# Routed rows packed into 64 tiles with 27 extra products, and a first stage with the constants loaded behind x, four parts of blocks and normalisation by ScalarE

## The reference, cut to what matters

```python
x = L0_attn_x                                  # (8, 1024, 128) f32: 8192 tokens
xn = layernorm(x)
# "attention": out = s * colsum(W_out) + b_out for each token
off = xn @ W_off + b_off                       # only the even columns are used
w = softmax((xn @ W_attn + b_attn).reshape(..., 8, 4), axis=-1)
idx = clip(where(int(off) < 0, int(off) + 128, int(off)), 0, 127)
s = sum(take_along_axis(xn[:, 0, :], idx) * w)
# feed forward: two shared experts for all tokens, two of eight for each token
ffn = lambda x, w1, w2, w3: (silu(x @ w1.T) * (x @ w3.T)) @ w2.T   # 128 -> 256 -> 128
logits = xn @ router_w.T + expert_bias
rw, sel = top_k(logits, 2); rw = softmax(rw)
routed = sum over the two chosen experts of rw * ffn(xn, expert)
return x + attention + shared + routed
```

## Time and profile before

| | us |
|---|---|
| median of 3 runs | 506.35 (503.58 to 506.4) |
| the profiled execution | 503.18, its span 501.4 |
| PE busy | 432.6 (86%) |
| DVE busy | 331.3 (66%) |
| POOL busy | 231.1 (46%) |
| ACT busy | 229.1 (46%) |
| stage 1, first normalisation to last copy | 16.7 to 61.1 |
| stage 2, to PE's first turn of stage 3 | 61.7 to 262.4 |
| stage 3, to the last product | 262.4 to 489.4 |
| last sends | to 501.4 |

### The profile page before, as it was taken

How to read it: one execution, slowest core, us unless ns; L and a number is a source line. 1 busy time by engine, 2 the same in 40 slices (tenths; PEclk the granted TensorE clock), 3 DMA queues, 4 the chain that set the end, 5 groups by cost and what they waited for, 6 DMA issues and landing times.

```text
span 501.4 us, 14718 instructions
## 1 busy us (share of the span) xinstructions
PE 432.6 (86%) x5200; PEld 376.1 (75%) x5200; DVE 331.3 (66%) x956; ACT 229.1 (46%) x432; POOL 231.1 (46%) x179
## 2 busy tenths in 40 slices
PE   0167676677899999999999999999999999999990
PEld 0156534354577777777788999999999999999990
DVE  3799799989768799999966776344434444344440
ACT  0588841163224544444443454444444444444440
POOL 0234400146754433333000000688888888887663
PEclk9999998999999999999998999999999999999995
DMA  8999400000331111111302432354444444432000
GB/s 238 284 171 174 74 1 1 5 32 18 99 112 34 54 44 55 48 43 48 96 2 96 140 110 95 75 59 64 63 55 66 55 60 60 60 37 23 4 2 1
DMA packets 50683, 34.58 MB, mean 69 GB/s; under 512 B 9408, under 2 KB 44224, under 8 KB 50624
## 3 DMA queue, kind: packets, MB, share of 16 engines
q1 hardware_dynamic: 32048, 23.88, 20.4%
q0 software_dynamic: 15296, 8.53, 12.4%
q10 hardware_dynamic: 3280, 1.36, 1.1%
HBM read 14.87 MB, written 20.69 MB: 71 GB/s over the span
## 4 chain that ended last, share of the span: by engine, by line
PE 72%; DVE 19%; issue 2%; ACT 2%; ACTq 2%; DMA 1%; POOL 1%; DVEq 0%; POOLq 0%
PE pY L616 17%; PE pY L466 9%; PE pAB L596 9%; PE pAB L598 8%; PE pAB L597 8%; PE pAB L451 4%; PE pAB L453 4%; PE pAB L452 4%; PE pV L491 3%; PE pV L478 3%; DVE units L894 3%; PE pV L579 2%; DVE hbuf L923 2%; DVE hot L834 2%; ACTq L630 2%
## 5 line engine op out<-in xcount | busy, mean ns | idle before, releaser
L798 POOL DMA_INDIRECT out_dram<-hot,rows x92 | 142.5, 1549 | 110.9 <-DVE hot L1173 86.0
L1167 DVE SCALAR_TENSOR_TENSOR hbuf<-pAB,units 128x512 f32<-128x512 f32 x92 | 63.6, 691 | 103.9 <-PE pAB L598 103.9
L596 PE MATMUL pAB<-xT,wsp 128*128 128x128 f16 x736 | 129.6, 220 | 1.1 <-ACT xT L737 0.6
L597 PE MATMUL pAB<-xT,wsp 128*128 128x128 f16 x736 | 129.7, 220 | 0.0
L598 PE MATMUL pAB<-xT,wsp 128*128 128x128 f16 x736 | 129.6, 220 | 0.0
L788 POOL DMA_INDIRECT sorted_rows<-rows,slot x64 | 69.4, 1084 | 112.2 <-DVE hbuf L923 64.4
L616 PE MATMUL pY<-wsp,hbuf 128*128 x736 | 103.0, 282 | 1.0 <-issue 0.7
L747 ACT ACTIVATE units<-pAB 128x512 f32<-128x512 f32 x92 | 55.0, 598 | 105.5 <-PE pAB L598 105.5
L616 PEld LDWEIGHTS pY<-wsp,hbuf 128*128 128x128 f32 x736 | 89.7, 192 | 1.7 <-issue 1.3
L701 ACT ACTIVATE units<-pAB 128x512 f32<-128x512 f32 x64 | 38.1, 597 | 113.8 <-PE pAB L453 113.8
L596 PEld LDWEIGHTS pAB<-xT,wsp 128*128 x736 | 72.5, 98 | 2.6 <-issue 2.1
(11 more groups left out here) (137 smaller groups left out, 558.0 us busy)
## 6 DMA issues: line engine op xcount, KB each, us to landing
sorted_rows<-c_pad_row SPq DMA_DIRECT2D x1, 6026.0 KB, 43.7
rows<-sorted_rows SPq DMA_DIRECT2D x46, 131.0 KB, 2.2
base<-in_x SPq DMA_DIRECT2D x4, 1024.0 KB, 8.2
out_dram<-base SPq DMA_DIRECT2D x16, 256.0 KB, 2.5
wraw<-in_wall SPq DMA_DIRECT2D x8, 256.0 KB
out_dram<-hot,rows POOLq DMA_INDIRECT x92, 3.3
sorted_rows<-rows,slot POOLq DMA_INDIRECT x64
wsp<-in_wall SPq DMA_DIRECT2D x8, 128.0 KB, 2.8
```

Source lines behind the costliest of these rows:

```text
L596: pe.matmul(o, hi, x(0), start=True, stop=False)
L597: pe.matmul(o, hi, x(1), start=False, stop=False)
L798: pool.indirect_dma_start(out_rows, bass.IndirectOffsetOnAxis(ap=xr[:, t // 2 % X_RING, t % 2, DEST:DEST + 1].bitcast(U32), axis=0), yt[:, ...
L1167: v.scalar_tensor_tensor(hbuf[:, r % 4, :], pAB[:, 2 * (r % 2) + 1, :], 1 / (XS * WS), silu[:, r % 2, :], ALU.mult, ALU.mult).then_inc(d_h ...
```

## The change

The pairs of experts are put in an order in which neighbours share an expert (RUNS). Segments are no longer rounded to tiles: the 8192 rows fill 64 tiles exactly, and a tile's two products are those of the pair that owns its first row. Where a new pair begins within a tile, its one expert that the pair before lacks (COMER) is computed for that whole tile by an extra product: 27 extras, two to a job, so 14 extra jobs beside 64 main ones. Jobs run in the order main 0 to 7, extras 0 to 13, main 8 to 63. A row carries the weights of all 8 experts (ROWW 137 in place of 131), and each tile's shares are formed from them by DVE. The results of all 64 tiles stay in SBUF, cleared by POOL, and an extra adds to the tile that a register names. Sends wait for the last extra. The pad write goes. ADDS is 2, and blocks are written at WRITE_AT, which puts the last one behind turn 24 (step 34 of 78).

In stage 1, x comes in 8 DMAs on SP, the other constants and the shared weights on SP behind it; ACT issues 3 DMAs. The parts of blocks are 0-1, 2-4, 5-9, 10-15. ACT normalises all four tiles of blocks 0 to 10, DVE the fourth of blocks 11 to 15. The shared weights' split moves to blocks 14 and 15.

```diff
-NQ = 4
+NQ = 8
-TILES = -(-((TOK + NPAIR * (P - 1)) // P) // 2) * 2
-STEPS = TILES // 2
+RUNS = [(0, 1, 8), (1, 7, 8), (1, 2, 7), (2, 6, 8), (2, 3, 6), (3, 5, 8), (3, 4, 5), (4, 5, 8), (5, 7, 8), (5, 6, 7), (6, 7, 8)]
+PAIRS = [(u, v) for u, lo, hi in RUNS for v in range(lo, hi)]
+EXTRAS = NPAIR - 1
+TILES = NT
+MAIN_STEPS = TILES // 2
+XTILES = (EXTRAS + 1) // 2
-PARTS = [(0, 4), (4, 8), (8, 16)]
+PARTS = [(0, 2), (2, 5), (5, 10), (10, 16)]
-ROOT_AT = {1: 1, 2: 6}
+ROOT_AT = {1: 1, 2: 4, 3: 9}
+FOURTH_FROM = 11
-ADDS = 3
-Y_RING, OUT_SEMS = 32, 8
+ADDS = 2
+EXTRA_FROM = 8
+JOBS = ([Job(t=t) for t in range(EXTRA_FROM)] + [Job(i=i) for i in range(XTILES)]
+        + [Job(t=t) for t in range(EXTRA_FROM, TILES)])
+WRITE_AT = [min(n for n in range(AHEAD, STEPS) if FIRST_OF_TURN[n - AHEAD + 1] >= TPB * (i + 1) // ADDS + 3) for i in range(NB)]
...
 SP
-            sp.wait_ge(const_in, 16 * n_const)
-            sp.dma_start(sorted_rows..., c["pad_row"]...).then_inc(pad_out, 16)
+                if q == NQ // 2 - 1:
+                    for r in range(2):
+                        sp.dma_start(wraw[:, r, 0:W2], wall[r, :, 0:W2]).then_inc(w_in[r], 16)
+            for dst, src in [(wo[:], w_out), (bo_raw[:], ...)] + [(c[k][:], const[k]) for k in const if k != "ident"]:
+                sp.dma_start(dst, src).then_inc(const_in, 16)
...
+            def load_extra(a, landed):
+                with sp.register(f"extra{a}") as tile:
+                    sp.reg_load(tile, segi[0:1, 1, a:a + 1])
+                    ...
+                    sp.dma_start(xe[:, a - 1], sorted_tiles[bass.ds(at, 1)]...).then_inc(landed, 16)
...
+            for n, step in enumerate(TURN_ORDER):
+                if n >= AHEAD:
+                    sp.wait_ge(d_turn, n + 1 - AHEAD)
+                if step < MAIN_STEPS:
+                    sp.dma_start(xr[:, step], sorted_steps[step]).then_inc(d_in[n % AHEAD], 16)
+                else:
+                    ...load_extra for its one or two extras
+                for i in range(NB):
+                    if n == WRITE_AT[i]:
+                        write_block(i)
...
 PE
+            def spread_sides():
+                pe.wait_ge(spread_ready, 1)
+                pe.wait_ge(y_read, NB)
+                for b in range(2):
+                    mm = pe.matmul(pY[:, b, :], c["ones"][:], spread..., start=True, stop=True)
+                mm.then_inc(sides_done, 1)
...r_turn: behind turn 0
+                if job.turn == 0:
+                    spread_sides()
...r_first, r_second: as before for a main job; for an extra job
+                                e = NSH + COMER[2 * job.i + k + 1]
+                                hi, lo = (wsp[:, s, e, col + h * P:col + (h + 1) * P] for s in range(2))
...
 ACT
-            act.wait_ge(const_in, 16 * n_const)
             root(0)
+            act.wait_ge(first_in, 16 * 3)
+            nc.scalar.activation(wp[:, 0, :], wp_raw[:], ACT.Copy, scale=WS).then_inc(wp_hi, 1)
-                for j in range(TPB - 1):
+                for j in range(TPB - 1 if i >= FOURTH_FROM else TPB):
-            pipeline(act, NB, 4, 4, [(0, normalise), (0, later_roots), (0, shared_high), (2, turned_copy)])
+            pipeline(act, NB, 4, 4, [(0, normalise), (1, shared_high), (2, turned_copy), (0, later_roots)])
...
-            pipeline(act, TILES, ..., [(0, r_xt), (5, r_y_first), (2, r_silu)])
+            pipeline(act, NJOB, ..., [(0, r_xt), (2, r_silu)])
...
 POOL
+            pool.wait_ge(cw_pair, 1)
+            for m, (choice, k) in enumerate(((5, 8), (4, 9))):
+                nc.gpsimd.tensor_tensor(r8[:, choice], r8[:, choice], rt[:, k, :]..., ALU.mult).then_inc(cw_part, 1)
+            pool.wait_ge(cw_part, 2)
+            nc.gpsimd.tensor_tensor(rows32[:, :, CW:CW + E], r8[:, 5], r8[:, 4], ALU.add).then_inc(cw_ready, 1)
...behind the scatter
+            for i in range(NB):
+                pool.wait_ge(l1, 4 * i + 4)
+                nc.gpsimd.memset(yt[:, TPB * i:TPB * (i + 1)], 0.0).then_inc(y_cleared, 1)
...r_send
-                pool.wait_ge(d_y, t + 1)
+                pool.wait_ge(d_y, max(job.place, LAST_EXTRA) + 1)
...
             pool.wait_ge(out_done, 16 * NB)
-            for step in range(SEND_FROM, TILES + 7): ...
+            for job in JOBS:
+                if job.main:
+                    r_send(job)
...
 DVE, routing: L991, L993 to L997 and six of L1001 to L1007 go; seven runs of L976 become eleven
-            then(v.scalar_tensor_tensor(tab_scr[:], ... [P, 2, NPAIR] ...
+            then(v.scalar_tensor_tensor(tab_scr, ... [P, 2 + 2 * E, NPAIR] ...
...at the end of stage 2: spread_out (one tensor_tensor of 1024), extra_table (seven small ones)
...
+            def load_tiles(g, r):
+                first = REG_LOAD * (UNROLL * g + r) + 1
+                ...values_load_multi_w_load_instructions(segi[0:1, 1, first:last], engines=(DVE,), ...)
+            def side_products(g, r): (for each pair of main tiles, one tensor_tensor 128 x 32)
+            def side_sums(g, r): (one tensor_reduce of it)
+            def extra_shares(g, r): (for each extra, one tensor_tensor 128 x 1)
+            def y_first(g, r):
+                ...
+                dve.wait_ge(d_l2, q + 1)
+                if job.main:
+                    dve.wait_ge(share_ready, job.step + 1)
+                    v.scalar_tensor_tensor(yt[:, job.t], pY[:, q % 2, 0:P], share_w[:, job.t, 0:1], yt[:, job.t],
+                                           ALU.mult, ALU.add).then_inc(y_half, 1)
+                else:
+                    row = yt[:, bass.ds(extra_tile[a], 1)].rearrange("p o c -> p (o c)")
+                    v.scalar_tensor_tensor(row, pY[:, q % 2, 0:P], extra_w[:, a:a + 1], row, ALU.mult, ALU.add)...
+            def y_second(g, r): (the same for the second half, behind y_half)
-            pipeline(dve, TILES, ..., [(0, r_attention), (5, r_y), (2, r_hf)])
+            pipeline(dve, NJOB, ..., [(5, y_first), (0, r_attention), (0, load_tiles), (2, side_products), (5, y_second), (2, r_hf),
+                                      (3, side_sums), (2, extra_shares)])
```

More of the change, by code:

```diff
@@ L79, with __init__, comes_back @@
 GAP_UNIT, SEG_UNIT, TAB_UNIT, TABLE_UNIT, LOGIT_UNIT, SIZE_UNIT = 3, 6, 10, 12, 12, 14
+SPREAD_UNIT = UNITS - 4
+REG_LOAD = 4
 PACE_FROM, PACE = 9, 50
-ADDS = 3
-Y_RING, OUT_SEMS = 32, 8
-X_RING, AHEAD = NT // 2, 8
-SEND_FROM = 24
+ADDS = 2
+AHEAD, OUT_SEMS = 8, 8
+EXTRA_FROM = 8
+class Job:
+    def __init__(self, t=None, i=None):
+        self.t, self.i = t, i
+        self.main = t is not None
+        self.step = t // 2 if self.main else MAIN_STEPS + i
+        self.turns = not self.main or t % 2 == 0
+        self.experts = 2 if self.main else min(2, EXTRAS - 2 * i)
+        self.cols = self.experts * HID
+JOBS = ([Job(t=t) for t in range(EXTRA_FROM)] + [Job(i=i) for i in range(XTILES)]
+        + [Job(t=t) for t in range(EXTRA_FROM, TILES)])
+NJOB = len(JOBS)
+TURN_ORDER = [job.step for job in JOBS if job.turns]
+for n, step in enumerate(TURN_ORDER):
+    for job in JOBS:
+        if job.step == step:
+            job.turn = n
+for q, job in enumerate(JOBS):
+    job.place = q
+FIRST_OF_TURN = [min(q for q in range(NJOB) if JOBS[q].turn == n) for n in range(STEPS)]
+WRITE_AT = [min(n for n in range(AHEAD, STEPS) if FIRST_OF_TURN[n - AHEAD + 1] >= TPB * (i + 1) // ADDS + 3) for i in range(NB)]
+LAST_EXTRA = max(job.place for job in JOBS if not job.main)
+LAST_OF_TURN = [max(q for q in range(NJOB) if JOBS[q].turn == n) for n in range(STEPS)]
+def comes_back(a):
+    return max([g for g in range(a) if COMER[a] in PAIRS[g]], default=-1)
 def constants():
@@ L570, in r_turn @@
                     return
-                j = UNROLL // 2 * g + r // 2
-                pe.wait_ge(d_in[j % AHEAD], 16 * (j // AHEAD + 1))
-                if j == 0:
+                rows_landed(pe, job.step)
+                if job.turn == 0:
                     pe.wait_ge(w_split, NE)
-                if past(j, 2):
-                    pe.wait_ge(d_xt, j - 1)
-                for k in range(2):
+                if job.turn >= 2:
+                    pe.wait_ge(d_xt, job.turn - 1)
+                for k in range(2 if job.main else job.experts):
@@ L635, in _ @@
-            act.wait_ge(const_in, 16 * n_const)
-            nc.scalar.activation(wp[:, 0, :], wp_raw[:], ACT.Copy, scale=WS).then_inc(wp_hi, 1)
-            nc.scalar.copy(bo[:], bo_raw[:]).then_inc(wp_hi, 1)
+            for dst, src in [(wp_raw[:], wproj), (c["ident"][:], const["ident"]), (bp[:], bproj)]:
+                act.dma_start(dst, src).then_inc(first_in, 16)
             def split_high(g, r):
@@ L871, in _ @@
-            scales(0)
-            for i in range(*PARTS[1]):
+            for i in (3, 4):
                 block_statistics(i)
+            variances(1)
             def later_parts(g, r):
                 i = 4 * g + r
-                if i == 0:
-                    variances(1)
-                if i == 2:
+                if i == 1:
```

(34 more changed lines are left out.)

434 lines of the change are left out of this document (269 added, 165 removed).

## The result

The changed kernel takes **483.62 us** (median of 4 runs, 482.18 to 484.47) against 505.59 for the kernel before on the same chip (4 runs, 503.58 to 506.4): ratio 0.9571, 95% interval 0.9544 to 0.9598. Forecast was 473, with 467 to 478 as its own range, and 464 to 485 with the rivals. The direction was right. The time lies 10.6 us above the forecast, outside its own range and at the slow end of the wide one. Its profiled execution took 484.23 us, 1.8 more than its span of 482.4.

A forecast was written before the change was run, and what follows sets the result against it. It took DVE to bound stage 2's routing, PE the rest of stage 2 and stage 3. Stage 3's start 259.9 + last send 201.3 + tail 8.65 = 469.9 span, 471.7 time; stated 473, range 467 to 478.

The forecast's parts named there:

- ACT becomes the bound of the stage: Stage 1: ACT's work and waits give back most of a 7.1 us earlier first normalisation; last copy ends at 58.95.
- 16 of some 0.7 us are covered: End of stage 2: POOL's 16 clears of about 0.7 us each, behind the last scatter, cost nothing.
- rival 2: Stage 3 before the first send: register loads and dynamic addresses make DVE the bound, +8 to +10, 482 us; chance 0.25.
- rival 3: Stage 3: SP's register reads and DMA issues bring extra tiles late, +5 to +10, 480 us; chance 0.05.
- Stage 3, PE: PE's time from first turn to last product of stage 3 falls from 227.0 to 193.9 us.
- S: The start of stage 3, its first turn on PE, forecast at 259.9 us.
- Stage 3, the sends: POOL's 64 sends start late, run back to back at 1.85 us and set the end, adding 4.1 us.
- DVE in stage 3: DVE's new step needs 1.95 of 2.40 us, so it fits with 0.45 to spare; register loads cost nothing.
- rival 5: Stage 3: extras serialise and give back a tile's time for each saved, no change, 503 us; chance 0.03.
- rival 1: Stage 3: PE still sets the end instead of POOL's sends, 465 to 469 us; chance 0.13.
- 2.2 gained: Stage 1: the last copy ends at 58.95 instead of 61.13 us; bounds 7 gained to 2 lost.
- Rival 4: Stage 3: DVE makes PE pause in each step and PE's clock falls to 1.2 GHz, 523 us; chance 0.04.

The follow-up runs named there:

- experiment 10: Changed kernel with POOL's constants' wait behind its subtractions, clears spread between scatters, three attention additions a step, and without the 27 extra products: 440.58 us, ratio 0.8724.
- experiment 4: Changed kernel with attention added to three tiles a DVE step instead of two, last block's write behind turn 18: 479.16 us, ratio 0.9488.
- experiment 1: Changed kernel with POOL's wait for all constants, and the destination column's copy, moved behind its stage 1 subtractions: 477.62 us, ratio 0.9445.
- experiment 2: Changed kernel with POOL's 16 clears spread between the scatters of the second half instead of back to back behind the last: 477.43 us, ratio 0.9454.
- experiment 3: Changed kernel with each POOL clear waiting for the one before, all still behind the last scatter: 477.63 us, ratio 0.9439.
- experiment 6: Changed kernel with POOL's constants' wait behind its subtractions, and DVE normalising the fourth tile of all 16 blocks again: 478.72 us, ratio 0.9465.
- experiment 7: Changed kernel with the 4.5 MB pad write put back and POOL's scatter waiting for it: 484.16 us, ratio 0.9584.

## Why the prediction was right, and where it failed

**The steps that failed are "ACT becomes the bound of the stage" in stage 1 and "16 of some 0.7 us are covered" in stage 2.** They put POOL's wait for the constants and its clears at nothing, and the runs show 5.9 and 6.5 us. That the wide range still held the time was luck: its upper part stood for rivals 2 and 3, which lie in stage 3 and did not happen, and two waits that the prediction does not name filled it. Stage 2 alone missed by 9.6 us, where its bounds allowed less than 2.

- **Stage 3, PE: right.** 193.9 us from S to the last product forecast, 194.4 measured. The 14 extra steps cost 2.40 us each by experiment 10.
- **Stage 3, the sends: right in kind, 1 us short in size.** The last block's write behind turn 24 did hold the first send (S + 84.65 forecast, 85.65 measured), all 64 went back to back, 116.7 us forecast for 63 intervals and 117.1 measured. POOL's queue cost 5.2 us (experiment 4), not 4.1; the tail behind it was 1.7 shorter. The chain of waits still shows PE with 64% and POOL with 2%: it steps onto PE wherever a send had just been released, so it names POOL for the last four sends only. The sends' rows show the backlog: all but the first have 0.30 us ahead of them.
- **DVE in stage 3: right.** The timeline of one step with extras, against the earlier trace rows:

```profile
304.76 0.69 DVE L1338 SCALAR_TENSOR_TENSOR hbuf<-pAB,units 128x512 f32<-128x512 f32 x1 [0.64 <-PE pAB L716]
305.37 0.22 DVE L1368 TENSOR_TENSOR hot<-proj,active 128x1 f32<-128x1 f32 x2
305.51 0.34 DVE L1389 SCALAR_TENSOR_TENSOR xT<-pY,hot,xT 128x128 f32 x1
305.77 0.60 DVE L1411 SCALAR_TENSOR_TENSOR base<-csum,attn_all,base 128x128 f32<-128x128 f32 x2
306.36 0.35 DVE L1405 SCALAR_TENSOR_TENSOR xT<-pY,hot,xT 128x128 f32 x1
307.27 0.69 DVE L1338 SCALAR_TENSOR_TENSOR hbuf<-pAB,units 128x512 f32<-128x512 f32 x1 [0.56 <-PE pAB L716]
```

  Step to step 2.51 us, 0.6 of it idle, released by PE. The register loads don't stand in this step but in the first seven. In the first three of those DVE idles 0.67, 0.49 and 0.55 us by "issue", so the 0.7 a step of rival 2 was about right as a price, but DVE had that time to spare: PE's last product came at S + 194.4 all the same. Rivals 2, 3 and 5 did not happen, and rival 1 did not either, by experiment 4.
- **Stage 1: the step "ACT becomes the bound of the stage" failed.** The first normalisation was on time, but I followed the moved constants only past ACT and SP. Of POOL I looked at the subtraction's duration and not at what stood ahead of it in its program. Its wait for all constants, harmless while they came first, now ended at 19.50 and held the first subtraction. Price: 5.9 us by experiment 1. With the wait gone ACT is the bound, but its sum was 2.6 too high, so the net miss was 3.2. The forecast "2.2 gained" became 1.0 lost.
- **Stage 2: the step "16 of some 0.7 us are covered" failed.** They did lie in POOL's free time, and at 0.5 us each; but covering asks also what they hold while they run. They held DVE's comparison and through it PE, 6.5 us by experiments 2 and 3 with the clock. The Trainium skill, SBUF — State Buffer, section "SBUF: two separate sides", has the rule: the shared pair of ports is an exclusive lock, and the loser fully blocks. By that section a DVE instruction with one input, as here, takes the pair only in a 2-port mode, and no row here shows the mode. I had weighed it for POOL's subtraction and its multiplications, and not for these. The trace agrees with the blocking, but not with its length: a lock held for one instruction would have cost one clear, about 0.5 us, as it does in experiments 2 and 3 (611 and 656 ns at the longest), and here it was 5843 ns.
- **Rival 4, the clock, did not happen where it was looked for.** I had looked for pauses in each step of stage 3; from 273 to 467 the clock is 1.00. The sign named for being wrong, 0.5 in more than one stretch, did come, ahead of S: in stage 1, where PE is not full and experiment 1 shows no price, in the routing, where it is part of the 1.0 us of experiment 2, and behind PE's pause at the end of stage 2 (0.50 for 252 to 256).
- **The routing: net 0.3 gained forecast, about 1 lost.** POOL's addition cost DVE's 0.95 us, which I had taken as 0.9. What I had not seen is a new wait: the six small operations of the segment table (1.3 us) went, and in their place DVE waits 1.60 us for PE's product, the row at 84.96; 0.6 of that is the lower clock, by experiment 2. Of the 9.2 us by which stage 2 grew, 6.5 are the clears and 1.2 the routing up to the first scatter; the other 1.5, behind the first scatter, are not traced to a step.
- **The fourth tile on ACT: a bound of up to 7 us, measured at 0.5** (experiment 6). **The pad write: nothing, right** (experiment 7).

The three steps that the forecast missed or left (wait, clears, first send) are three small edits. With them and the earlier roots the kernel runs at 463.05 us, 0.9157 of before, nearly twice the gain of the change as it stands (43 us against 22).

## What to carry to other kernels

When a transfer moves back in a queue, list every engine that waits for it, and what each has in its program behind that wait; an engine in order pays for a wait that belongs to an instruction needed much later. Work "in the free time of an engine" is covered only if it holds nothing that others use: on POOL, put a wait or other work between its instructions when DVE has the critical path. Removing work from PE shows in the time only as long as the serial queue of sends behind it can start earlier as well.

## What the hardware showed that I had not expected

- POOL's 15 clears of 128x512 f32 without a wait between them kept one DVE instruction out for 5843 ns; the same with a semaphore wait between each two, 656 ns. DVE had not got its turn at the borders of single instructions.
- A clear reads no tensor, and still held DVE's one-input comparison.
- DVE's two-input addition of 1792 elements took 2.98 us against 2.03 alone: 0.95 longer, where POOL's two-input addition had 1.10 us left to run when it started. Where DVE's started 0.46 us ahead (experiment 2) it was POOL's that took 2.94 instead of 1.27.
- After PE's pause of 4.65 us the granted clock was 0.50 from 252 to 256; without the pause it was 1.00 from 230 to 262.
